# Feed-forward, third block: residual tiles turned in banks of their own and added by VectorE

## The reference

```
h = x                                # here x is layernorm of the part's input
for blk in range(3):
    y = qlora_linear(h, weights 2*blk)       # dequantised weight, bias, LoRA
    y = layernorm(y, gamma[blk], beta[blk])
    y = gelu(y)
    y = qlora_linear(y, weights 2*blk + 1)
    h = y + h
return h                             # and the caller adds the part's input
```

## Time and profile before

| | |
|---|---|
| median of three runs | 5513.49 us (5511.73 to 5526.04) |
| the profiled execution | 5511.73 us, its span 5509.5 us |
| PE busy in the span | 5255.2 us (95%) |
| VectorE busy | 2593.6 us (47%) |
| ScalarE, GpSimd busy | 1691.8 us (31%), 1285.7 us (23%) |
| mean granted clock of PE | 0.982 of full speed |
| the third block's PE work | 1637.3 to 1883.3 us, with step 16's transposes from 1621.8 |

### The profile page before, as it was taken

The page is one execution under the profiler, slowest core; times in us unless marked ns, Lnnn a source line. Parts: engine busy times, 40 slices in busy tenths (PEclk is TensorE's granted clock), DMA queues, the critical chain, the costliest instruction groups (busy, mean ns, idle before and its releaser), DMA issues. The chain is left out here.

```text
span 5509.5 us, 76305 instructions
## 1 busy us (share of the span) xinstructions
PE 5255.2 (95%) x26230; PEld 2626.4 (48%) x26230; DVE 2593.6 (47%) x4158; ACT 1691.8 (31%) x2290; POOL 1285.7 (23%) x965
## 2 busy tenths in 40 slices
PE   8999989999999899899978998699999999999999
PEld 4444446644445444445444555544444444444444
DVE  4243237654343322355532665655555555455554
ACT  1001015522211100234321443144444344444443
POOL 1000015511112100000011222433333333333333
PEclk9999999999999999999999999899999999999999
DMA  1010021230012223699975113587877836746546
GB/s 57 8 50 5 16 75 52 83 85 22 20 31 69 100 97 124 155 220 216 219 201 202 39 54 114 189 301 247 280 265 264 281 87 224 250 131 236 175 137 227
DMA packets 438992, 772.24 MB, mean 140 GB/s; under 512 B 64962, under 2 KB 208583, under 8 KB 438293
## 3 DMA queue, kind: packets, MB, share of 16 engines
q1 hardware_dynamic: 377620, 725.42, 40.9%
q0 software_dynamic: 34304, 44.13, 4.2%
q10 hardware_dynamic: 26880, 0.19, 0.3%
HBM read 577.35 MB, written 116.79 MB: 126 GB/s over the span
## 5 line engine op out<-in xcount | busy, mean ns | idle before, releaser
L2877 PE MATMUL ex_ps<-ex_w,ex_xT 128*64 128x512 f32 x5376 | 1226.6, 599 | 19.6 <-DVE ex_w L2760 19.5
L2760 DVE COPY ex_w<-ex_shelf 128x4096 f32 x336 | 770.1, 2292 | 520.3 <-PE ex_ps L2877 382.4
L2811 ACT ACTIVATE ex_w<-ex_shelf 128x4096 f32 x168 | 607.9, 3619 | 1043.4 <-PE ex_ps L2893 1028.8
L2877 PEld LDWEIGHTS ex_ps<-ex_w,ex_xT 128*64 128x64 f32 x5376 | 373.2, 137 | 655.5 <-issue 609.6
L2893 PE MATMUL ex_ps<-ex_w,ex_hT 128*64 128x256 f32 x5376 | 610.9, 380 | 5.6 <-ACT ex_hT L2827 3.8
L2730 POOL DMA_INDIRECT out<-ex_y,ex_ix_out x168 | 287.7, 1713 | 1179.2 <-DVE ex_ix L2748 805.8
L2893 PEld LDWEIGHTS ex_ps<-ex_w,ex_hT 128*64 128x64 f32 x5376 | 390.2, 137 | 270.1 <-issue 99.1
L2713 POOL DMA_INDIRECT ex_x<-moe_xn,ex_ix x168 | 412.2, 2454 | 86.3 <-issue 51.2
L1533 PE MATMUL ff_ps<-ff_w,ff_hT 128*128 128x512 f32 x768 | 349.3, 598 | 6.7 <-DVE ff_y L1414 3.9
L1725 PE MATMUL pr_ps<-pr_w,pr_xT 128*128 128x512 f32 x768 | 334.5, 593 | 0.8 <-ACT pr_xT L225 0.8
L1482 ACT ACTIVATE ff_gT<-ff_ps,ff_bet,ff_gam 128x128 f32<-128x128 f32 x384 | 143.9, 459 | 459.0 <-PE ff_ps L1543 459.0
(11 more groups left out here) (281 smaller groups left out, 6922.2 us busy)
## 6 DMA issues: line engine op xcount, KB each, us to landing
ex_shelf<-L_ffn_w SPq DMA_DIRECT2D x128, 2048.0 KB, 14.1
ex_shelf<-L_ffn_wo SPq DMA_DIRECT2D x64, 2048.0 KB
cv_gt<-cv_g SPq DMA_DIRECT2D x320, 128.0 KB, 3.8
cv_vt<-cv_v SPq DMA_DIRECT2D x256, 128.0 KB, 5.8
ff_x<-x SPq DMA_DIRECT2D x16, 1024.0 KB, 8.1
at_low<-x SPq DMA_DIRECT2D x8, 1024.0 KB, 5.8
x<-at_acc SPq DMA_DIRECT2D x8, 1024.0 KB, 4.2
xa_x<-x SPq DMA_DIRECT2D x8, 1024.0 KB, 8.8
```

Source lines behind the costliest of these rows:

```text
L2760: dve.tensor_copy(w_s[n][:, :], pick(shelf[n], buf)).then_inc(w_set[n].sem, 1)
L2811: act.activation(w_s[2][:, :], pick(shelf[2], buf), ACT.Copy).then_inc(w_set[2].sem, 1)
L2877: mm = pe.matmul(ps[q * G:(q + 1) * G, which, 0:FQ], xT[:, p % 2, k, :], wu[which][:, k, q * FQ:(q + 1) * FQ], start=k == 0, stop=k == KD - 1)
```

## The change

In the third block product1 only multiplies. The tiles of hT are turned by real transposes (`turn_h`) into banks 6 and 7, one tile at the head of each round j of a step, ahead of turn_g. VectorE adds bank 6 or 7 to xn (`add_h`) in its own round j, behind moments and normal of the next step, and evict then adds the product as before. Two semaphores order this: h_mm (turned) and h_done (added, bank free). turn_h of the block's first tile waits for all dequantised weights, whose LoRA products use the same banks, and for the last update of hT. The wait for base moves from evict to add_h, and evict waits for h_done, which VectorE itself has counted up before.

```diff
+        last_part = lambda s, u: part(s - (NB - 1) * NC, u)
@@ evict, third block
-                    if u == 0:
-                        dve.wait_ge(base_done, c + 1)
+                    dve.wait_ge(h_done, last_part(s, u))
                     o = xn[:, c % 2, u, :]
                     dve.tensor_tensor(o, bank, o, ALU.add).then_inc(o_done, 1)
+
+            def add_h(s, j):
+                c = s % NC
+                dve.wait_ge(h_mm, last_part(s, j))
+                if j == 0:
+                    dve.wait_ge(base_done, c + 1)
+                o = xn[:, c % 2, j, :]
+                dve.tensor_tensor(o, ps[:, 6 + j % 2, :], o, ALU.add).then_inc(h_done, 1)
@@ VectorE's loop
                         moments(s + 1, j)
                         if j:
                             normal(s + 1, j - 1)
+                    if s >= (NB - 1) * NC:
+                        add_h(s, j)
@@ product1
-                        pe.matmul(bank, gT[:, s % 2, k, u * P:(u + 1) * P], w[:, b % 2, 1, k, :], start=k == 0, stop=False)
-                if b == NB - 1:
-                    for k in range(KD):
-                        i = pe.matmul(bank[:, k * P:(k + 1) * P], hT[:, k, span(s, u)], ident[:, :], start=False, stop=k == KD - 1)
+                        i = pe.matmul(bank, gT[:, s % 2, k, u * P:(u + 1) * P], w[:, b % 2, 1, k, :], start=k == 0, stop=k == KD - 1)
                 i.then_inc(o_mm, 1)
+
+            def turn_h(s, j):
+                n = last_part(s, j)
+                if n == 1:
+                    pe.wait_ge(w_done, 2 * KD * NB)
+                    pe.wait_ge(o_done, part((NB - 1) * NC - 1, TJ - 1))
+                if n > 2:
+                    pe.wait_ge(h_done, n - 2)
+                for k in range(KD):
+                    i = pe.transpose(ps[:, 6 + j % 2, k * P:(k + 1) * P], hT[:, k, span(s, j)], ident[:, :])
+                i.then_inc(h_mm, 1)
@@ PE's loop
+                    if s >= (NB - 1) * NC:
+                        turn_h(s, j)
                     if s >= 0:
                         turn_g(s, j)
```

More of the change, by code:

```diff
@@ L1262, in stage_ffn @@
         base_done = st.sem("base_done")
+        h_mm = st.sem("h_mm")
+        h_done = st.sem("h_done")
         stored = [st.sem("stored0"), st.sem("stored1")]
```

## The result

Fifteen runs of each kernel on the same chip: 5529.51 us median (5519.88 to 5539.72) against 5515.57 (5511.73 to 5526.04). The ratio is 1.0023, 95% interval 1.0016 to 1.0030: about 13 us slower. The change takes work off PE, and the kernel gets slower by almost as much as the work was worth (15.8 us by the prediction's sum).

A forecast was written before the change was run, and what follows sets the result against it. TensorE, 95% busy, bounds the kernel by its order of work. Costs of 30.9 us less 15.8 gain give +15.1 on 5511.73, so 5526.8; the median lies 1.8 higher: 5528.5 us, range 5517 to 5537.

The forecast's parts named there:

- a tile's turn; gain over 28 tiles: TensorE, steps 16 to 22: turning an hT tile takes 0.44 us instead of 0.89, saving 12.7 us.
- step 23, product1 later by the first turn: Last step of the third block: only the first turn, 0.44 us, stands ahead of the first gelu; 3.1 us saved.
- step 16, wait for the last w: Start of the third block: TensorE newly waits 2.3 us for all dequantised weights, with no clock loss.
- steps 17 to 21, arrival to release: TensorE at turn_h(s, 3) waits for add_h(s, 1), queued behind a normal needing GpSimd's base: 16.2 us in all.
- step 22, arrival to release: Same wait at turn_h, with base later behind early loads: 9.7 us, replacing today's wait of 3.6.
- clock, steps 17 to 21: TensorE's granted clock falls after four of the five waits, at 1.6 us each: 6.4 us.
- clock, step 22: Lower TensorE clock after step 22's long wait costs 1.7 us; 1.8 of today's loss is given back.
- clock, step 23: Left as before: product1 comes out of the last gelu wait slowly, 6.04 us where 3.60 is usual.
- block: Stretch from step 15's last LoRA products to the next stage's first transposes; the forecast's net was +15.1 us.
- Every wait paying: Rival: all seven TensorE waits, step 16's included, lose clock: +18.9 us, 5532.4 us; chance 0.20.
- The covered wait: Rival: x loads early enough that base frees GpSimd before TensorE reaches turn_h(s, 3): 5500 us, to 5495; chance 0.10.
- turns cost double: Rival: turning hT costs as much as the product with the identity, 8 records: 5533.5 us; chance 0.04.

The follow-up runs named there:

- the second run: The change as it is, measured once more against the kernel before: ratio 1.0020 (1.0011 to 1.0029), block 277.3 us.

## Why the prediction was right

| term of the sum | forecast | measured in the profile |
|---|---|---|
| a tile's turn; gain over 28 tiles | 0.44; 12.7 us | 0.43 to 0.44 |
| step 23, product1 later by the first turn | 0.44 us | 6.82 for 6.38 us: 0.44 |
| step 16, wait for the last w | 2.3 us | 2.3 (from the step's start) |
| steps 17 to 21, arrival to release | 16.2 us | 3.38, 3.53, 3.27, 3.14, 3.26: 16.6 |
| step 22, arrival to release | 9.7 us | 8.7 |
| clock, steps 17 to 21 | 6.4 us, four of five | 6.5, four of five; 0 in the second run |
| clock, step 22 | 1.7 us | 2.1; 3.0 in the second run |
| clock, step 23 | as before, 2.4 us | 1.8; 0.1 in the second run |
| block | +15.1 us | +14.4, +7.0 in the second run |

Distances here are counted as in the prediction, from the step's start; the idle column of a row reads 0.16 less, as records overlap. The clock of steps 17 to 22 is what the work from turn_h to product1 took above the 4.36 us of step 20, that of step 23 what its first products took above their usual time.

*The mechanism* was read from the trace of before, and every link of it held: arrival at + 12.93, release at base + 6.58. That VectorE had room for 22 us of additions was true, and not the question; the place in its queue was. Moving add_h by one place shows it, and moving PE's arrival by 3.9 us shows it from the other side.

*Step 22* was a microsecond too dear: base started 15.03 us behind the step's start, for 16.09 in the trace of before. The load was issued equally late (4.4 us) in both and landed a microsecond sooner; the second run had a wait of 9.09.

*The clock* is the term that I could not have had right. Its bounds for each wait, nothing and 1.8 us, were both all but met (0 and 1.7), in two executions of the same kernel; four of five was luck. Step 23 was left as it was, and the runs show it to vary too: behind a wait of 2.07 us for the gelus the first products lost 1.8 to 2.4 us in six of the eight profiles that have it, and 0.1 in two. That a wait of 1.8 us or less costs nothing and one from 2.69 on may cost was read from too few rows, since that 2.07 stood in the trace of before with its loss. From runs whose waits agree to tenths of a microsecond, what it costs on average can only be had from the times: a ratio worth 13 us (11 in the second measurement), against a block 7.0 us longer with no fall in steps 17 to 21 and 14.4 with four. How often it falls isn't shown.

*The rivals.* Every wait paying (5532.4) fell at once: step 20's 2.97 and step 16's 2.17 paid nothing. The covered wait (5500) didn't come about, for the reason given: base still starts past 9.4. It names what makes the change a gain, though: PE's arrival against the release. In the runs above one or the other was moved, and the kernel came out at 0.996 to 0.998. That turns cost double fell on the first row of the table.

*The chances* had 0.48 on within 0.3% and 0.42 on slower; the measured 0.23% lies in the first, and with a share of luck: the blocks of two executions of the same code differ by 7.4 us, half the effect. Luck is also in 5528.5 against 5529.51: the median of the kernel before moved up by 2.1 us from three runs to fifteen, and the difference itself was 13 to 14 us for 15.1. In the block (+14.4 for +15.1) step 22's wait was a microsecond too high, its clock 0.4 too low and step 23's 0.6 too high.

## What to carry to other kernels

An instruction moved off the busiest engine onto one with room to spare is not free if the busy engine must then wait for it: ask what stands ahead of it in the other engine's queue, and whether anything there waits for a third engine or for a load. Work out two times from the start of a step, when the busy engine arrives and when the other releases it; here 12.9 against 16.0 us decided between 13 us lost and 15 to 16 gained, and one piece of work moved in either engine's order closed it. When a slow piece is moved to cover a wait, look at what runs on the engine beside it at the new place.

## What the runs showed of the hardware

- Waits of 3.10 to 3.37 us on TensorE were followed by 1.4 to 1.7 us of lost pace in one execution, and one of 3.31 us by none in another, at the place where 3.37 had paid. A wait of 2.16 us paid once in six profiles, one of 2.07 us behind shorter ones in six of eight.
- With float32 transposes to nowhere in place of the waits the granted clock was 1.00 over 200 us; of the waits replaced only the one of step 22 (8.51 and 9.09 us when empty) was followed by the lower clock in both profiles of the change.
- VectorE's tensor_scalar over 128x512 from SBUF takes 0.52 us, and 4.72 when it starts beside GpSimd's tensor_tensor of 4.50 us; one that started inside such an instruction ended 0.3 us after it. The bias addition at 1634.77, which reads PSUM and SBUF, took its usual 0.69 us inside base.
- Turning a float32 tile of 128x512 takes 0.44 us as four transposes and 0.89 us as four products with the identity.
